# Second attention layer: value products in bursts of three pieces, six probability buffers, PSUM as four T banks and two S banks instead of two and four

## The reference, cut to what matters

```python
q_blhd = jnp.einsum('bld,dhk->blhk', x_bld, Wq)
latent_bll = jnp.einsum('bld,dc->blc', x_bld, Wkv_down)
k_blhd = jnp.einsum('blc,chk->blhk', latent_bll, Wk_up)
v_blhd = jnp.einsum('blc,chk->blhk', latent_bll, Wv_up)
attn = jnp.einsum('bqhd,bkhd->bhqk', q_blhd, k_blhd) / jnp.sqrt(HD)
attn = jax.nn.softmax(jnp.where(mask, attn, neg_inf), axis=-1)
y_blhd = jnp.einsum('bhqk,bkhd->bqhd', attn, v_blhd)
return jnp.einsum('bqhd,hdo->bqo', y_blhd, Wout)
```

## Time and profile before

| | us |
|---|---|
| median of 3 runs | 2335.16 (2334.02 to 2335.99) |
| the profiled execution | 2343.62 |
| its span, first to last instruction | 2341.9 |
| second attention, first T to the last copy of O | 1270.0 to 1924.0 |
| busy in the span: TensorE | 2097.0 (90%) |
| busy in the span: VectorE | 1542.6 (66%) |
| busy in the span: ScalarE | 1373.8 (59%) |
| busy in the span: GpSimd | 487.9 (21%) |

### The profile page before, as it was taken

How to read it: one execution, slowest core, us unless ns; L and a number is a source line. 1 busy time by engine, 2 the same in 40 slices (tenths; PEclk the granted TensorE clock), 3 DMA queues, 4 the chain that set the end, 5 groups by cost and what they waited for, 6 DMA issues and landing times. The chain is left out here.

```text
span 2341.9 us, 43593 instructions
## 1 busy us (share of the span) xinstructions
PE 2097.0 (90%) x10732; PEld 1351.8 (58%) x10732; DVE 1542.6 (66%) x6216; ACT 1373.8 (59%) x2513; POOL 487.9 (21%) x808
## 2 busy tenths in 40 slices
PE   3479999999963999999977999999999997499998
PEld 2245555555533788888733555555555547378886
DVE  4378778877825677777755666666666633567776
ACT  1236666666653889999842555555555565355554
POOL 4101111111103000000000111111111110266665
PEclk9779999999995999999986999999999998599999
DMA  3533334333301221122166555555555521076552
GB/s 95 175 51 54 53 46 60 51 50 50 46 22 63 55 55 37 37 45 45 18 234 186 127 118 117 117 121 128 128 128 117 117 46 58 25 157 120 132 122 60
DMA packets 96650, 202.81 MB, mean 87 GB/s; under 512 B 14496, under 2 KB 32160, under 8 KB 96032
## 3 DMA queue, kind: packets, MB, share of 16 engines
q1 hardware_dynamic: 96544, 201.65, 38.8%
HBM read 169.47 MB, written 31.60 MB: 86 GB/s over the span
## 5 line engine op out<-in xcount | busy, mean ns | idle before, releaser
L575 DVE CUSTOM_DVE_ANT_0 a1ms<-a1S,mask_q 128x128 bf16<-128x128 f32 (+1 forms) x758 | 387.8, 553 | 182.6 <-issue 179.1
L629 ACT ACTIVATE a1p<-a1T 128x512 f32<-128x512 f32 x576 | 331.4, 597 | 293.9 <-PE a1T L731 293.4
L575 DVE CUSTOM_DVE_ANT_0 a0ms<-a0S,mask_q 128x384 bf16<-128x384 f32 (+2 forms) x752 | 379.7, 553 | 109.6 <-issue 108.2
L629 ACT ACTIVATE a0p<-a0T 128x512 f32<-128x512 f32 x576 | 330.0, 597 | 188.7 <-PE a0T L731 177.8
L710 PE MATMUL a1O<-a1p,a1v 128*33 128x512 f32 (+3 forms) x1536 | 304.3, 496 | 1.0 <-POOL a1p L543 0.9
L731 PE MATMUL a0T<-a0qT,a0kT 128*128 128x512 f32 (+3 forms) x768 | 265.4, 392 | 18.3 <-DMA a0qT<-a0mr 6.8
L1184 DVE TENSOR_TENSOR m_hl<-m_h,m_hh 128x512 fp32r<-128x512 f32 x288 | 197.7, 690 | 116.8 <-ACT m_hh L1140 111.7
L731 PE MATMUL a1T<-a1qT,a1kT 97*128 97x512 f32 (+3 forms) x768 | 262.8, 390 | 0.7 <-DMA a1qT<-a1mr 0.7
L670 PE MATMUL a0S<-a0kS,a0qS 128*128 128x384 f32 (+2 forms) x752 | 229.0, 361 | 27.9 <-DMA a0kS<-scr_k 21.7
L731 PEld LDWEIGHTS a1T<-a1qT,a1kT 97*128 97x128 f32 x768 | 131.6, 189 | 200.7 <-ACT a1p L629 144.5
L670 PE MATMUL a1S<-a1kS,a1qS 96*128 96x128 f32 (+1 forms) x758 | 220.6, 353 | 13.0 <-DMA a1kS<-scr_k 12.8
(11 more groups left out here) (234 smaller groups left out, 3628.3 us busy)
## 6 DMA issues: line engine op xcount, KB each, us to landing
m_gb<-scr_g SPq DMA_DIRECT2D x48, 1024.0 KB, 8.6
a1qS<-scr_q SPq DMA_DIRECT2D x96, 256.0 KB, 6.1
a1qT<-scr_q SPq DMA_DIRECT2D x96, 256.0 KB, 4.0
a1kS<-scr_k SPq DMA_DIRECT2D x96, 128.0 KB, 6.8
a1kT<-scr_k SPq DMA_DIRECT2D x96, 128.0 KB, 4.7
scr_q<-p_hi SPq DMA_DIRECT2D x32, 256.0 KB, 2.5
scr_q<-p_lo SPq DMA_DIRECT2D x32, 256.0 KB, 2.7
a0qS<-scr_q SPq DMA_DIRECT2D x48, 128.0 KB
```

Source lines behind the costliest of these rows:

```text
L575: nc.vector.tensor_tensor_reduce(masked_s[spare][:, 0:c1 - c0], buf[:, 0:c1 - c0], k.mask_q[:, SEQ - w + c0:SEQ - w + c1], 1.0, NEVER, ALU ...
L629: nc.scalar.activation(prob_of(g, p)[:, h, :], t_ps[slot % 2][:, :], ACT.Exp, scale=scale)\
```

## The change

The second attention is called with `BURST=3, TBUF=4`; the first keeps its values.

- `BURST=3`: the value products of three pieces follow one another. They stand in slot 7 (pieces 0 to 2), slot 13 (pieces 3 to 5) and slot 1 of the next group (pieces 6 to 8). O's first bank is then copied out at slot 14 instead of 12.
- `PBUF` becomes 2 x 3 = 6 probability buffers instead of 3.
- `TBUF=4`: T takes turns through four banks, and T of a slot waits for the exponential of four slots back, not two.
- `BANKS` becomes (6 - 4) x 2 / 2 = 2. A unit waits for the unit two back, not four back. The ring at the start of the stage, which also uses O's banks, has four banks, not six; VectorE's scratch `masked_s` has two buffers instead of four.
- The last line looks up the earlier user of a bank in a longer list; for a ring of four it finds the same one.

```diff
-def attention(k, name, HG, VD, scale, operands, load_q, load_k, load_v, out, PARTS=1, BURST=1, HALVES=2):
+def attention(k, name, HG, VD, scale, operands, load_q, load_k, load_v, out, PARTS=1, BURST=1, HALVES=2, TBUF=2):
...
-    BANKS = 2 * HALVES
+    BANKS = (6 - TBUF) * HALVES // 2
+    assert 2 * NSLOT % TBUF == 0
...
-        t_ps = [c.enter_context(nc.psum_tensor(name + f"T{i}", [P, ST], F32)) for i in range(2)]
+        t_ps = [c.enter_context(nc.psum_tensor(name + f"T{i}", [P, ST], F32)) for i in range(TBUF)]
...
-                            nc.scalar.activation(prob_of(g, p)[:, h, :], t_ps[slot % 2][:, :], ACT.Exp, scale=scale)\
+                            nc.scalar.activation(prob_of(g, p)[:, h, :], t_ps[(g[1] * NSLOT + slot) % TBUF][:, :], ACT.Exp, scale=scale)\
...
-                            if not (at(g, 0) and slot < 2):
+                            if not (at(g, 0) and slot < TBUF):
 
-                                pe.wait_ge(exp_done, lin(g, NSLOT, slot - 1))
+                                pe.wait_ge(exp_done, lin(g, NSLOT, slot - TBUF + 1))
...
-                                last = nc.tensor.matmul(t_ps[slot % 2][:, off:off + q1 - q0],
+                                last = nc.tensor.matmul(t_ps[(g[1] * NSLOT + slot) % TBUF][:, off:off + q1 - q0],
...
-                    unit(units_from([("o", 0, 0, 0)]), before(END)[HALVES:], main_ring(unit_slot(END) + HALVES), n, END)
+                    unit(units_from([("o", 0, 0, 0)]), (before(END) + units_of(END))[HALVES:], main_ring(unit_slot(END) + HALVES), n, END)
...
-                attention(k, "a1", 2, 32, 64.0 ** -0.5, rows, split_rows(q1, 2, 32, (0, 0, 1)), load_k1, load_v1, attn)
+                attention(k, "a1", 2, 32, 64.0 ** -0.5, rows, split_rows(q1, 2, 32, (0, 0, 1)), load_k1, load_v1, attn, BURST=3, TBUF=4)
```

## The result

The change makes the kernel slower: 2563.04 us median (2558.68 to 2580.02, 4 runs) against 2335.57, a ratio of 1.097 with a 95% interval of 1.0929 to 1.1012. The sign was forecast, the size was not: 2477 us with a range to 2540. The profiled execution took 2560.78 us against 2343.62, so +217.2, and it is this difference that the trace can explain.

The account below looks back on a forecast made before the run. TensorE's instruction stream was taken as the bound. A group goes from 20.48 to 18.5 us by fewer switches, then to 25.1 by 6.6 of waits; 30 x 4.65 + 2.5 = +142 on 2335.2 gives 2477 us, range 2425 to 2540.

Parts of the forecast that it names:

- What bounds the kernel now: Second attention, steady part: TensorE's instruction stream is the bound, 20.48 us a group, and the four-bank ring costs it nothing.
- The ring of two: Units of the second attention wait for VectorE's read two units back: a loss, new waits of 6.6 us a group.
- A, B and C: Intervals between bursts: slots 2 to 7, 8 to 13, and 14 to 17 with 0 and 1; 5.75, 5.35, 5.95 us.
- pull-ahead of loads: Weight loads passing a bank's wait would shorten a group by some 2 us, to about 23; the sum left it out.
- The intervals here resemble the tail more than the fall: Intervals likened to the first attention's tail, full clock at 8.64 of 10 us busy, not a fall after 1.85 of 3.4.
- the clock rival: Gaps between bursts drop TensorE to half clock: about 2705 us, or 2553 if in one interval of three; chance 0.09.
- Fewer switches: Value products in bursts of three save TensorE six switches a group: a gain of 2.0 us (1.5 to 2.1).
- T banks and probability buffers: Four T banks and six buffers in the second attention: worth nothing, since ScalarE needs only 11.2 us of a group.
- Edges: Start and last two groups of the second attention's stage: together +2.5 us.

Follow-up runs that it names:

- ring of two alone: Four T banks and two banks for the units, but BURST=1 and three probability buffers, against the kernel before: 2516.5 us, ratio 1.0764.
- half reads: The whole change, with VectorE reading only the first half of each S unit's columns: 2424.9 us, ratio 1.0359 against the kernel before.
- shorter exponentials: BURST=3 with two T banks and four unit banks, ScalarE's exponential over half the columns: 2338.5 us, ratio 1.002 against the kernel before.
- shorter reads: BURST=3 with two T banks and four unit banks, exponentials and VectorE's maxima both over half the columns: 2312.1 us, ratio 0.9867 against the kernel before.
- three and three banks in bursts: BURST=3 with three banks for T and three for the units, against the kernel before: 2387.8 us, ratio 1.0231.
- burst alone: BURST=3 with six probability buffers, but still two T banks and four unit banks, against the kernel before: 2354.5 us, ratio 1.0058.

## Why the prediction was wrong

**What bounds the kernel now: right.** TensorE's stream, with the four-bank ring free: the ring of two alone costs 5.9 us a group.

**The ring of two: right, to 0.2 us a group.** Laid out were 5.75, 5.35 and 5.95 us for A, B and C and 2.69 for a burst; at full clock they took 5.67, 5.27, 6.09 and 2.70. The group of 25.1 us is met in every second group. In the others the turn of the loop, which is hidden in the kernel before (its groups take 20.48 and 20.46 in turn), adds about 0.4 us; it was no term of the sum. With it the waits are 145 us, where 139.5 were laid out. The half reads bear out the mechanism, and a waiting S load starts 0.05 us past the end of VectorE's read (order of time after the change):

```profile
1505.07 0.08 DVE L576 DVE_READ_ACCUMULATOR2_ANT a1mh<- 128x1 f32 x1
...
1505.20 0.19 PEld L671 LDWEIGHTS a1S<-a1kS,a1qS 96*128 96x128 f32 x1 [0.59 <-DVE a1held L573]
```

So the pull-ahead of loads that the Trainium skill describes ("TensorE: Matmul & The Clock Gate", opening table) did not reach past a bank's wait here.

**The step that failed: "The intervals here resemble the tail more than the fall, and each is followed by a dense burst", and with it the clock at 1.00 and a chance of 0.09 for the clock rival.** The clock fell 43 times. This missing term is 2.4 us a group, 72 us, and it alone puts the time outside of the range: without it 2563 would be 2491. The comparison was made by busy time: 8.64 of 10 us in the first attention's tail. Interval C shows nearly the same, 5.16 of 6.09, and the clock fell behind it; the ring of two alone shows 472 of 540 and it never fell. The busy share doesn't separate the cases. One reason can be that a matmul that starts on an idle TensorE is booked with 0.50 us, while one in a stream is followed by the next after 0.23 to 0.25. In the tail the gaps alternated with dense products every 3.1 us; here the bursts stood 5 to 6.5 us apart. The rival was priced at 2553 for a fall in one interval of three; it was more like one in two, mostly after C and B, each worth about 1.65 us where 2.5 was put down. The rule of the Trainium skill ("TensorE: Matmul & The Clock Gate", "A second HAM failure mode: psum-queue depth-cycling"), weighed against it, was the better guide for this kernel: with bursts this trace agrees (43 falls), with the ring of two alone it does not (none).

**Fewer switches: the sign was right, the size too large.** 2.0 us a group forecast, about 1.3 measured. A further piece in a burst does take 0.86 us instead of 0.99; going in and out costs less than the 0.20 that I put down. It had no part in the error of the total, because the intervals were laid out directly.

**T banks and probability buffers "worth nothing": right only beside a ring of two.** With the ring of four the two T banks pace part of the burst version (20.7 against 20.3 us a group with shorter exponentials), so more than two T banks would have been of use there; how many, no run shows. For VectorE three banks cost bursts 22.2 us a group, and even with four the shorter reads still gained 1.1 us (20.3 to 19.2). No split of the six banks that was run serves both.

**Edges:** the stage grew by 218.2 us, of which 145 + 72 are 217, so the +2.5 for the edges can't be told from the rounding of these terms.

**Open:** what exactly of an interval brings the clock down. Filling the gaps takes the falls away (43, 10, 6, 1 with 0, 5, 8 and 24 matmuls more a group), and so does a shorter interval C: at 6.1, 5.2, 5.0 and 4.7 us (change, half reads, three and three banks in bursts, burst alone) there were 43, 7, 2 and, in groups with S units, no falls. This shows that the long thin intervals are the cause; where the border lies was not settled. No version here that computes the reference beats the kernel before.

## What to carry to other kernels

Before work is put in bursts, count what the other engines can hold in banks during a burst: here they stood idle for the rest, and then paced what lay between. With two banks for a producer and a consumer, the producer's latency and the consumer's read were in series here, and both durations belong in the sum; the step from three banks to two was eight times that from four to three. Where a change thins TensorE's work out between bursts, put a price on half clock (72 of 217 us here), and don't judge it by TensorE's busy share. Where the order of work is a loop over two groups, its turn belongs in the sum too once nothing hides it: about 0.4 us in every second group here, nothing before.

## What the runs showed of the hardware

The clock fell behind stretches in which TensorE counts as busy for 85% (5.16 of 6.09 us), and held 1.00 through 540 us with 87% (472.08), where products of 0.98 us stood after every second slot and not in bursts. Matmuls that compute nothing new kept the clock up: with five more a group the kernel was 49 us faster than without them. One fall of 3.4 us cost about 1.65 us of time where it lay in a burst, and 1.2 us with half reads, where it began before the burst.
